# The opening of a pre-norm attention and feed-forward kernel: TensorE turns the identity over first, shorter rounds of the inverse root, the second chunk normed alone

## What is computed

```python
x = x + attention(layernorm(x))      # 16 heads, 16 "splats" a head
x = x + ffn(layernorm(x))
# layernorm: (x - mean) / sqrt(var + 1e-5) along the 256 numbers of a row
# attention: q, k, v = x @ qkv_w.T
#   weights_q[s] = exp(-0.5 * |q - center_s|^2 / scale_s^2), the same for k
#   logits = sum_s weights_q[s] * weights_k[s] * amplitude_s;  softmax;  @ v;  @ out_w.T
# ffn: r = sigmoid(mix_r(x) @ W_r.T);  k = relu(mix_k(x) @ W_k.T)^2;  r * (k @ W_v.T)
#   mix(x) = mu * x + (1 - mu) * (x one row earlier)
```

## Time and profile before

| | us |
|---|---|
| median of 3 runs | 2230.28 |
| lowest and highest | 2228.0, 2232.36 |
| the profiled execution's own time | 2232.91 |
| its span, first to last instruction | 2231.1 |
| outside the span | 1.8 |
| mean granted TensorE clock | 0.996 |

### The profile page before, as it was taken

One profiled execution on the slowest core, in us unless ns is written; L12 is line 12 of the kernel. 1 busy time (PEld: TensorE's weight loads), 2 busy tenths in 40 slices (PEclk: granted clock), 3 DMA queues, 4 the chain that ended last, 5 costly groups with the idle time before them and its releaser, 6 DMA issues.

```text
span 2231.1 us, 47336 instructions
## 1 busy us (share of the span) xinstructions
PE 2160.7 (97%) x20406; PEld 912.8 (41%) x20406; DVE 894.0 (40%) x1769; ACT 2005.9 (90%) x2194; POOL 389.3 (17%) x490
## 2 busy tenths in 40 slices
PE   6899999999999999999999999999999999999998
PEld 4433443343443434434344343443444444433445
DVE  5244334435335353443624435244343333323336
ACT  3699999999989898999999899898999999998995
POOL 0242423330220220303012022220400000000001
PEclk9999999999999999999999999999999999999999
DMA  5654325324231331512532223321333131210111
GB/s 146 170 142 99 96 62 135 88 74 132 56 114 42 94 105 35 129 49 56 138 93 71 75 75 90 93 83 36 98 91 79 33 72 42 58 38 28 42 39 38
DMA packets 172804, 180.37 MB, mean 81 GB/s; under 512 B 84992, under 2 KB 110976, under 8 KB 172576
## 3 DMA queue, kind: packets, MB, share of 16 engines
q1 hardware_dynamic: 163312, 162.32, 26.6%
q0 software_dynamic: 7168, 14.69, 2.9%
q10 hardware_dynamic: 2096, 0.14, 0.1%
HBM read 86.45 MB, written 75.89 MB: 73 GB/s over the span
## 4 chain that ended last, share of the span: by engine, by line
PE 74%; ACT 21%; DVE 3%; issue 1%; POOL 1%; DMA 1%; SPq 0%; DVEq 0%; POOLq 0%
PE ps_pv L759 32%; PE ps_scores L740 21%; ACT probs L1073 20%; PE ps_step L787 16%; PE ps_step L804 2%; PE ps_scores L772 1%; ACT weight L1137 1%; DMA gate_in<-x 1%; PE ps_scores L777 1%; DVE den_all L1530 0%; PE ps_step L766 0%; POOL packed L1208 0%; PE ps_scores L782 0%; PE ps_scores L781 0%; DVE mixed_r L1398 0%
## 5 line engine op out<-in xcount | busy, mean ns | idle before, releaser
L1073 ACT ACTIVATE probs<-ps_scores 128x1024 f32<-128x1024 f32 x2048 | 1931.9, 1043 | 156.1 <-PE ps_scores L740 151.7
L759 PE MATMUL ps_pv<-probs,vals 128*32 128x512 f32 (+1 forms) x8712 | 1069.8, 580 | 4.3 <-DVE o_raw L1415 2.0
L740 PE MATMUL ps_scores<-q_aug,k_aug 49*128 49x512 f32 x4096 | 718.3, 440 | 31.4 <-ACT probs L1073 24.1
L740 PEld LDWEIGHTS ps_scores<-q_aug,k_aug 49*128 49x128 f32 x4096 | 333.6, 185 | 683.9 <-ACT probs L1073 642.2
L759 PEld LDWEIGHTS ps_pv<-probs,vals 128*32 128x32 f32 x8712 | 300.3, 141 | 285.4 <-issue 184.3
L1203 POOL DMA_DIRECT2D packed<-qk x224 | 112.4, 507 | 785.6 <-DVE qk L1348 750.3
L1208 POOL TENSOR_TENSOR packed<-qk 32x512 f32<-32x512 f32 x224 | 236.2, 1054 | 16.9
L1530 DVE RECIPROCAL den_all<-den_all 128x512 f32<-128x512 f32 x63 | 210.9, 3347 | 0.8
L1213 POOL TENSOR_TENSOR k_act<-k_act 128x512 f32<-128x512 f32 x28 | 30.4, 1085 | 970.8 <-DVE k_act L1351 970.8
L1415 DVE COPY o_raw<-ps_pv 128x512 f32<-128x512 f32 x64 | 44.3, 692 | 308.1 <-PE ps_pv L759 308.1
L1348 DVE COPY qk<-ps_step 128x512 f32<-128x512 f32 x56 | 38.7, 690 | 225.9 <-PE ps_step L787 225.9
(11 more groups left out here) (208 smaller groups left out, 1053.8 us busy)
## 6 DMA issues: line engine op xcount, KB each, us to landing
k_aug<-k_parts SPq DMA_DIRECT2D x128, 192.0 KB, 5.1
q_aug<-q_parts SPq DMA_DIRECT2D x128, 192.0 KB
k_parts<-parts SPq DMA_DIRECT2D x32, 512.0 KB, 3.4
q_parts<-parts SPq DMA_DIRECT2D x32, 512.0 KB, 3.3
packed<-qk POOLq DMA_DIRECT2D x224, 64.0 KB, 2.3
x_ffn<-x SPq DMA_DIRECT2D x18, 512.0 KB, 4.5
k_parts<-parts SPq DMA_DIRECT2D x32, 256.0 KB, 4.0
q_parts<-parts SPq DMA_DIRECT2D x32, 256.0 KB, 4.0
```

The lines of the kernel that those rows point to most:

```text
L740: mm = pe.matmul(ps_scores[:, g % RING, e, :], k_aug[rows, s % 2, pair, kt * P:(kt + 1) * P], q_aug[rows, u % 2, pair, :], start=True, sto ...
L759: mm = pe.matmul(ps_pv[32 * c:32 * c + 32, at], vals[:, s % 2, kt, :, c], probs[:, tick % PROB_SLOTS, c, at], start=(kt == 0), stop=(kt == ...
L1073: act.activation(probs[:, tick % PROB_SLOTS, 2 * pair:2 * pair + 2, :], ps_scores[:, g % RING, :, :], ACT.Exp).then_inc(probs_ready, 1)
```

## The change

Three edits, and the counts of the semaphores that follow from them:

- TensorE, which waits for the normed chunk 0, first issues 22 transposes of the identity as soon as the identity is there. They write the first 128 columns of the PSUM bank `ps_step`, which nothing reads before it is written again.
- A round of `newton` has 3 instructions in place of 4: y\*y, then (that \* -0.5) \* v, then (that + 1.5) \* y. The last two are `scalar_tensor_tensor`, with two operations and an immediate number each. So a norm's rounds are 9 instructions and not 12.
- Chunk 1 of the prologue has a semaphore of its own for its load (`second_x_loaded`) and for its norm (`second_ln`). VectorE norms chunk 1 alone when it has come, then chunks 2 and 3 together. The DMAs and their order stay.

```diff
-LN_STEPS = 4 + 4 + 3 + 4 * NEWTON + 4
-FIRST_LN_STEPS = 12 + 12 + 3 + 4 * NEWTON + 12
+LN_STEPS = 4 + 4 + 3 + 3 * NEWTON + 4
+FIRST_LN_STEPS = 8 + 8 + 3 + 3 * NEWTON + 8
+SECOND_LN_STEPS = 4 + 4 + 3 + 3 * NEWTON + 4
+WARM = 22
...
-            for i in range(1, NC):
+            sp.dma_start(out=first_x[1], in_=x_rows_of(x, 0, 1)).then_inc(second_x_loaded, 16)
+            for i in range(2, NC):
                 sp.dma_start(out=first_x[i], in_=x_rows_of(x, 0, i)).then_inc(first_x_loaded, 16)
...
                     pe.wait_ge(prep_ln, LN_STEPS)
+                elif i == 1:
+                    pe.wait_ge(second_ln, SECOND_LN_STEPS)
                 else:
...
+            pe.wait_ge(ident_loaded, 16)
+            for _ in range(WARM):
+                pe.transpose(ps_step[:, 0:P], ident[:, :], ident[:, :])
             first_turn(0)
...
                 for _ in range(rounds):
                     v.wait_ge(steps_sem, n.total())
-                    v.tensor_tensor(ln_a, ln_y, ln_v, ALU.mult).then_inc(steps_sem, n.step())
+                    v.tensor_tensor(ln_a, ln_y, ln_y, ALU.mult).then_inc(steps_sem, n.step())
                     v.wait_ge(steps_sem, n.total())
-                    v.tensor_tensor(ln_a, ln_a, ln_y, ALU.mult).then_inc(steps_sem, n.step())
+                    v.scalar_tensor_tensor(out=ln_a, in0=ln_a, scalar=-0.5, in1=ln_v, op0=ALU.mult, op1=ALU.mult).then_inc(steps_sem, n.step())
                     v.wait_ge(steps_sem, n.total())
-                    v.tensor_scalar(ln_a, ln_a, -0.5, 1.5, ALU.mult, ALU.add).then_inc(steps_sem, n.step())
-                    v.wait_ge(steps_sem, n.total())
-                    v.tensor_tensor(ln_y, ln_y, ln_a, ALU.mult).then_inc(steps_sem, n.step())
+                    v.scalar_tensor_tensor(out=ln_y, in0=ln_a, scalar=1.5, in1=ln_y, op0=ALU.add, op1=ALU.mult).then_inc(steps_sem, n.step())
...
-            first_layernorms()
+            first_layernorms((1,), second_x_loaded, second_ln)
+            first_layernorms((2, 3), first_x_loaded, first_ln)
```

More of the change, by code:

```diff
@@ L449, in preln_block @@
         first_x_loaded = sem("first_x_loaded")
+        second_x_loaded = sem("second_x_loaded")
         first_ln = sem("first_ln")
+        second_ln = sem("second_ln")
         first_mm = sem("first_mm")
@@ L1266, in layernorm @@
                 if part == 2:
-                    newton(ln_v[:, :], ln_y[:, :], ln_a[:, :], steps_sem, Count(base + 15), NEWTON - 1)
+                    newton(ln_v[:, :], ln_y[:, :], ln_a[:, :], steps_sem, Count(base + 14), NEWTON - 1)
                 if part == 3:
@@ L1274, in layernorm, with first_layernorms @@
                     assert n.total() == base + LN_STEPS
-            def first_layernorms():
-                stats, moments, ln_v, ln_y, ln_a = ln_tiles["first"]
+            def first_layernorms(chunks, loaded, steps_sem):
+                tiles = [(i, t) for i in chunks for t in range(TT)]
+                at = slice(TT * (chunks[0] - 1), TT * (chunks[-1] - 1) + TT)
+                stats, moments, ln_v, ln_y, ln_a = (tile[:, at] if len(tile.shape) == 2 else tile[:, at, :] for tile in ln_tiles["first"])
@@ L1279, in first_layernorms @@
                 n = Count(0)
[L1280 to L1295, removed]
+                v.wait_ge(loaded, 16 * len(chunks))
@@ new lines, in first_layernorms @@
+                for k, (i, t) in enumerate(tiles):
+                    v.bn_stats(out=stats[:, k, :], in_=first_x[i][:, t, :]).then_inc(steps_sem, n.step())
+                v.wait_ge(steps_sem, n.total())
+                for k in range(len(tiles)):
+                    v.bn_aggr(out=moments[:, k, :], in_=stats[:, k, :]).then_inc(steps_sem, n.step())
+                rsqrt_seed(moments, ln_v, ln_y, ln_a, steps_sem, n)
+                newton(ln_v, ln_y, ln_a, steps_sem, n, NEWTON)
+                v.wait_ge(steps_sem, n.total())
@@ L1297, in split @@
+                for k, (i, t) in enumerate(tiles):
+                    v.tensor_scalar(first_x[i][:, t, :], first_x[i][:, t, :], moments[:, k, 0:1], ln_y[:, k:k + 1],
+                                    ALU.subtract, ALU.mult).then_inc(steps_sem, n.step())
+                assert n.total() == (SECOND_LN_STEPS if len(chunks) == 1 else FIRST_LN_STEPS)
             def split(side, half, n):
```

## The result

The changed kernel takes 2221.61 us (median of 6 runs, 2220.47 to 2223.49). The kernel before, run beside it, takes 2229.75 (6 runs, 2228.0 to 2232.36). The ratio is 0.9963, with a 95% interval of 0.995 to 0.9976, so the change gains 8.1 us; 6.8 were forecast. The profiled execution took 2222.17, with a span of 2220.4 and a mean granted clock of 0.998; that of before took 2232.91. So the profiled executions lie 10.7 apart, 2.6 more than the medians. The experiments bear on where that comes from.

A forecast was written before the change was run, and what follows sets the result against it. TensorE (97% busy) was taken as the bound, except in the first 25 us, where it waits for VectorE. Prologue 5.2, other norms 1.5 and closing 0.1 made 6.8 us: 2223.5 us, range 2219.8 to 2227.8.

The forecast's parts named there:

- VectorE's rounds: Root of each norm on VectorE: three instructions fewer, 0.17 us for each new one, so a norm ends 0.6 us early.
- rival 2: Prologue: VectorE becomes the bound, the new instruction taking 0.25 us; gain 4.3 us, total 2226; chance 0.06.
- The 22 transposes: TensorE before the first turn: 0.217 us apart, from 5.6 to 10.6, ending 0.35 us before the turn, so costing nothing.
- rival 4: Start of TensorE's queue: the transposes hold up the first turn and make the kernel slower, 2234.8 us; chance 0.04.
- What they buy: Prologue on TensorE: transposes raise the clock to 2.4 GHz by 10.97, so chunk 1's turn comes at 19.8, 5.4 us early.
- Rival 1: Prologue: transposes do not raise the clock, so 2.85 us is gained there in place of 5.4; total 2225.8; chance 0.16.
- Late next: Constants on VectorE after chunks 2 and 3: they give back 0.2 of the 5.4 us, leaving 5.2 for the prologue.
- The other norms: 28 later norms, 0.6 us shorter each: three TensorE waits cut, at most 1.8 us, taken as 1.5.
- The closing stretch: End of the kernel: the last norm gains 0.1 us, since the next product needs GpSimd's square, which does not move.
- The sum: Whole kernel: 5.2 + 1.5 + 0.1 = 6.8 us gained, from the median of 2230.28 to 2223.5.
- rival 3: TensorE's clock falls more or less often: one more fall gives 2226.9 us, one less 2220.1; chance 0.12, half of it upward.
- The fall at 2041: Low clock of 6.8 us at 2041.6, costing at most 3.4; the stall ahead may be one that a norm ends.

The follow-up runs named there:

- old rounds: The changed kernel with four instructions a `newton` round as before, keeping the 22 transposes and the separate norm of chunk 1: 2228.29 us, ratio 0.999.
- the repeat: The changed kernel itself, unaltered, run once more in a later batch: 2221.85 us, ratio 0.9965.
- holds: The changed kernel with 14, 16 and 22 more identity transposes at three standstills of TensorE: 2219.75 us, ratio 0.9953.
- transposes alone: The kernel before with only the 22 transposes added ahead of its first turn: 2232.3 us, ratio 1.0008.
- chunk 1 alone: The kernel before with only chunk 1 normed separately, no transposes, four instructions a round: 2230.63 us, ratio 1.0001.
- chunk 1 alone with holds: The kernel before with chunk 1 normed separately and transposes at three standstills of TensorE, none at the start, four-instruction rounds: 2228.73 us, ratio 0.9993.
- the kernel before with holds: The kernel before with only 14, 16 and 22 transposes at three standstills of TensorE, no block ahead of the first turn: 2227.55 us, ratio 0.9988.

## Why the prediction was right, and where its size was off

*VectorE's rounds.* 0.17 an instruction was taken and 0.16 measured, so rival 2 (0.25) is out. The norm of chunk 0 ended 0.60 earlier, as forecast.

*The 22 transposes.* Forecast 5.6 to 10.6, measured 5.57 to 10.52. In three other executions of the same block (old rounds, the repeat, holds) it took 4.29, 4.12 and 3.93, since the clock rose within it. Either way they end before the first turn: rival 4 is out for 22.

*What they buy.* Forecast: first turn 10.97, product 12.85, values 16.35, turn of chunk 1 19.8. Measured: 10.98, 12.83, 16.37, 19.82. Rival 1, that transposes do not raise the clock, is refuted in every kernel with 22 or 44 of them: the first turn runs at the upper level, with no product before it. The Trainium skill ("TensorE: Matmul & The Clock Gate", "Part 4: PE-mode transpose") says that the high clock does not engage for transposes; the runs here, with transposes of float32, disagree, with a rise at 8.3 to 11.1 us for 16.8 to 19.2 without them. The prediction came to the right side from a row that did not prove it: that a stretch with transposes alone kept the clock says little, since the stall of 1.87 ahead of k of chunk 3 lost it in one execution and kept it in the next. The value of the edit, 5.4 - 2.85 = 2.55 by the prediction, is 2.29 in the profiles with holds and 3.55 in those without; the prediction had put the rise without transposes at a fixed 17.5.

*Late next.* 0.2 was to be given back at the constants; the bound was copied at 27.35, not 27.46, and the prologue was 5.35 early behind it, for 5.2. At the first unit's end with no falls 5.06 is left (there the load of chunk 3 had landed 0.34 earlier than in the profile of before). The term was right to 0.15.

*The other norms.* 1.5 was forecast. With holds on both sides the lead grows by 0.2 up to unit 42, by 0.6 at unit 43 and by 0.6 at unit 59: 1.4, so two waits were cut by the full 0.6 and not three. TensorE's waits for VectorE fell by 1.9, and 0.5 of that did not reach the end. The closing stretch gave 0.0 for 0.1, by the mechanism that the prediction had priced: GpSimd's square comes last.

*The sum.* 6.8 was forecast; 6.3 (runs) to 6.45 (profiles) is what the change is worth where the clock does not fall. The medians differ by 8.1: the kernel before is 3.6 above the runs without a fall (2229.75 for 2226.1), the changed kernel 1.9 (2221.61 for 2219.75), and 6.3 + 3.6 - 1.9 = 8.0. That is a way of dividing the 8.1 and no proof; that the clock is what lies between is borne out by the granted clocks of the runs, 0.997 before, 0.998 after and 1.000 in the runs without a fall. So the forecast of 6.8 was right in its terms, and the 1.3 that the medians differ by beyond it came through the clock and was not forecast.

*The step that was mis-sized* is rival 3. The prediction gave "the clock falls more, or less, often" a chance of 0.12, as an exception beside a forecast in which it stays the same, and looked for it at 2041 alone. It is not an exception. The fall at 2041 went, as the prediction had thought possible, one at 48.65 came that no row of before showed, and those of 70 to 100 changed their length. In these kernels the falls moved the medians by 0 to 4 us, as much as an edit, and single executions by more (the profile of before is 6.8 longer than that with holds). What a fall costs was bounded well, at half its length (1.70 measured for 3.41 at 48.65; 2.9 to 3.0 for 6.83 at 2041), with one fall a little over it (1.9 for 3.41 at 1246.59).

*The fall at 2041* looks like more than chance, if one takes all profiles together. The stall ahead of it ends with a norm, and lasts 1.8 us with the old rounds and 1.2 with the new ones. Of the six profiles with old rounds four have the fall (before, transposes alone, chunk 1 alone, chunk 1 alone with holds); of the eight with new rounds none has it. The runs with holds point the same way: with new rounds the granted clock is 1.000 in 11 of 11 runs, with old rounds in 4 of 22. So the shorter rounds seem to be worth up to 3 us more than the prediction's 1.5, through the clock, and a part of the 3.6 above may be theirs. This is a count over kernels that differ in other things too; a kernel with that one stall changed was not made.

*Left open.* Why the falls between 45 and 100 us lie where they do was not settled: the repeat shows that one program has them in different places. Nor was it tried which of the three holds is the one that matters.

## What to carry to other kernels

The gains of an opening do not simply add: TensorE's clock was worth 2.3 us or more only once the separate norm of chunk 1 had made TensorE the bound, and nothing before. When an edit moves stalls by a few us, compare at a mark before the first fall of the granted clock (here the turn of chunk 1, or the first exponential), and take the total only from versions whose clock does not fall. And a standstill of TensorE that leads to a fall can be filled with transposes into a free PSUM bank. In the changed kernel that gave 1.9 us and took the spread out of the time; in the two kernels with old rounds, whose stall ahead of 2041 us was left as it was, most runs still had falls.

## What the hardware showed that I had not expected

- Transposes of float32 alone raise the granted clock from 1.2 to 2.4 GHz (22 or 44 from 5.5 us: at the upper level by 8.3 to 11.1 us) and hold it: none of the kernels with 22 or 44 ahead of the turn ran it at the lower level. Ten of them, followed by a standstill of 3.0, did not raise it.
- The rise without them is not at a fixed time: 17.5, 17.7, 17.8 and 19.0 us where the first turn was at 11.6, and 16.8, 18.0 and 19.2 where it was at 10.8 to 11.0.
- Most of the spread of this kernel's time goes with the clock. With no fall and the 22 transposes five runs lie within 0.16 us; with falls eleven runs of one kernel lie over 2.3 to 7.9 us, and in the kernel before with holds the mean granted clock of a run (1.000, 0.999, 0.998) sorts them in steps of 1.6 and 1.4 us. It does not sort them everywhere: with 10 transposes, two runs at 2223.2 and eight near 2226 have the same 0.998.
